# Two cross-attention prologues: the value projections of chunk 1 and its key casts move in among the row maxima of chunk 0, and the order of the clock-keeping matmuls changes

## The reference

```
q = layernorm(x) @ Wq + bq;  k = ctx @ Wk + bk;  v = ctx @ Wv + bv
attn = softmax(clip(q k^T * 16**-0.5, -1e4, 1e4))      # per head, over 12544 keys
x = x + (attn @ v) @ Wo + bo
```

## Time and profile before

| | us |
|---|---|
| median of three executions | 1392.23 |
| the profiled execution | 1387.69 |
| its span, first to last instruction | 1385.9 |
| TensorE busy in it | 1216.7 (88%) |
| VectorE, ScalarE, GpSimd busy | 716.0, 712.6, 224.6 |
| share of the chain that ended last: TensorE, VectorE, DMA | 73%, 16%, 5% |

### The profile page before, as it was taken

One profiled execution on the slowest core, in us unless ns is written; L12 is line 12 of the kernel. 1 busy time (PEld: TensorE's weight loads), 2 busy tenths in 40 slices (PEclk: granted clock), 3 DMA queues, 4 the chain that ended last, 5 costly groups with the idle time before them and its releaser, 6 DMA issues.

```text
span 1385.9 us, 29435 instructions
## 1 busy us (share of the span) xinstructions
PE 1216.7 (88%) x12725; PEld 784.6 (57%) x12725; DVE 716.0 (52%) x1348; ACT 712.6 (51%) x991; POOL 224.6 (16%) x118
## 2 busy tenths in 40 slices
PE   8799999999999988315899799999999999988556
PEld 6256666666666655315697256666566666555345
DVE  2546555555555563577222545555555555563431
ACT  3246666666666657152113256666666666657110
POOL 0222222222222200041000222222222222200000
PEclk9689999999999999558799799999999999999568
DMA  8969777777777660610706969777777777660803
GB/s 146 135 84 122 95 95 95 99 93 97 99 96 95 76 150 2 217 53 27 277 1 106 131 92 126 96 88 97 97 91 97 96 97 95 75 117 2 326 11 55
DMA packets 85155, 140.31 MB, mean 101 GB/s; under 512 B 9112, under 2 KB 76384, under 8 KB 84512
## 3 DMA queue, kind: packets, MB, share of 16 engines
q1 hardware_dynamic: 84128, 138.29, 63.9%
q10 hardware_dynamic: 896, 0.12, 0.1%
HBM read 60.05 MB, written 0.18 MB: 43 GB/s over the span
## 4 chain that ended last, share of the span: by engine, by line
PE 73%; DVE 16%; DMA 5%; issue 2%; ACT 2%; POOL 0%; SPq 0%; ACTq 0%; DVEq 0%; POOLq 0%
PE ring L547 40%; PE st L547 16%; PE ot L547 15%; DVE mpart L1202 8%; DMA qst<-rowb 3%; DVE arena L1329 2%; PE ring L678 1%; DMA arena<-scratch_perm 1%; DVE arena L1333 1%; ACT arena L921 1%; PE ring L553 0%; DMA warena<-ctxT 0%; PE ring L646 0%; DVE work L1323 0%; POOL arena L536 0%
## 5 line engine op out<-in xcount | busy, mean ns | idle before, releaser
L1202 DVE TENSOR_REDUCE mpart<-ring 128x1 f32<-128x448 f32 x896 | 516.7, 621 | 435.2 <-PE ring L547 432.8
L944 ACT ACTIVATE work<-st 128x1024 f32<-128x1024 f32 x392 | 400.8, 1022 | 197.7 <-PE st L547 193.1
L547 PE MATMUL ring<-arena,qst 96*128 96x448 bf16 x896 | 299.8, 369 | 4.9 <-DVE mpart L1202 2.7
L547 PE MATMUL st<-qst,arena 97*128 97x128 bf16 x3136 | 245.0, 221 | 19.5 <-DMA qst<-rowb 18.2
L547 PE MATMUL ot<-work,arena 128*17 128x128 f32 x6272 | 250.4, 277 | 8.9 <-issue 6.7
L547 PEld LDWEIGHTS st<-qst,arena 97*128 97x128 bf16 x3136 | 199.0, 99 | 84.3 <-issue 31.9
L547 PEld LDWEIGHTS ot<-work,arena 128*17 128x17 f32 x6272 | 138.5, 97 | 151.3 <-issue 103.7
L499 POOL TENSOR_TENSOR arena<-arena 128x896 f32<-128x896 f32 x52 | 98.2, 1888 | 715.6 <-ACT arena L917 715.6
L547 PE MATMUL ring<-warena,wkv 96*128 96x448 f32 x448 | 195.4, 566 | 2.0 <-DVE mpart L1202 1.3
L547 PE MATMUL ring<-wkv,warena 96*128 96x256 f32 x784 | 190.2, 385 | 0.9 <-DVE mpart L1202 0.8
L547 PEld LDWEIGHTS ring<-wkv,warena 96*128 96x128 f32 x784 | 147.4, 191 | 28.4 <-DVE mpart L1202 11.1
(11 more groups left out here) (269 smaller groups left out, 645.3 us busy)
## 6 DMA issues: line engine op xcount, KB each, us to landing
arena<-arena SPq DMA_DIRECT2D x336, 224.0 KB, 11.4
warena<-ctxT SPq DMA_DIRECT2D x28, 672.0 KB, 13.3
arena<-ffn_W SPq DMA_DIRECT2D x16, 1024.0 KB, 12.4
arena<-f SPq DMA_DIRECT2D x2, 4096.0 KB, 24.4
arena<-scratch_bc SPq DMA_DIRECT2D x1, 2048.0 KB, 6.7
arena<-scratch_perm SPq DMA_DIRECT2D x2, 1024.0 KB, 10.2
arena<-rows SPq DMA_DIRECT2D x1, 1792.0 KB, 7.0
warena<-w_in_proj SPq DMA_DIRECT2D x1, 1024.0 KB
```

Of the source, the lines that this page charges most:

```text
L547: return nc.tensor.matmul(o, l, r, start=start, stop=stop, **kw)
L944: nc.scalar.activation(pbuf[:, n % 2], st[:, 2 * (n % 2):2 * (n % 2) + 2].rearrange("p b k -> p (b k)"), ACT.Exp).then_inc(*signal(f"{lay} ...
L1202: V.reduce_max(mpart[:, 2 * h + hf:2 * h + hf + 1], ring[:, BANKS[step][0], 0:HALF], AX_X).then_inc(*signal(f"{lay}_b_max"))
```

## The change

Three edits. The number of warm-up matmuls becomes 4 ahead of the transposition in both layers (16 before); behind it 12 in L0 (2 before) and 2 in L1 (as before). In the list the value steps of chunk 1 and the casts of its keys, which stood ahead of all maxima of chunk 0, are placed behind 5, 10, 15 and 20 of these; the last cast is placed behind 24. The remaining maxima of chunk 0 (the eight left) follow as before.

```diff
-WARM = (16, 2)
+WARM = (4, 12)
...
-    plan += [("v", 0, n) for n in range(4)] + [("k", 1, n) for n in range(4)] + [("v", 1, n) for n in range(4)]
-    plan += [("k1", 1, 0), ("k1", 1, 1), ("k2", 1, 0), ("k2", 1, 1)]
+    plan += [("v", 0, n) for n in range(4)] + [("k", 1, n) for n in range(4)]
+    for part in ([("v", 1, 0), ("k1", 1, 0)], [("v", 1, 1), ("k2", 1, 0)], [("v", 1, 2)], [("v", 1, 3), ("k1", 1, 1)]):
+        plan += some(5, 0) + part
+    plan += some(4, 0) + [("k2", 1, 1)]
     plan += some(2 * H, 0) + [("row", 0, 0)] + [("k", 2, n) for n in range(3)] + score(0) + [("k", 2, 3)] + score(1)
...
                 keep_clock(WARM[0])
                 transpose2(xn, 0, f"{lay}_ln_normed", f"{lay}_xT_full")
-                keep_clock(WARM[1])
+                keep_clock(WARM[1] if lay == "L0" else 2)
```

## The result

The changed kernel is slower: 1397.3 us median of 11 runs (1390.21 to 1404.61) against 1391.83 of 11 runs of the kernel before, a ratio of 1.0046 with the interval 1.0028 to 1.0064. The forecast was 3.9 us faster; it came out some 6 us slower, above the range's end of 1393.2.

What follows compares the result with a forecast made beforehand. The prologues were bound by projections before the maxima, the maxima, and a 4 KB row transfer of 12.5 us. L0 -1.6 and L1 -2.3 gave -3.9: 1383.8 profiled, 1388.3 as the median; range 1384.5 to 1393.2.

Steps and rivals of the forecast that it cites:

- The start of the maxima: Chunk 0's first maximum in each prologue: at 32.0 in L0 and 760.2 in L1, after a wait for the stack.
- Its neighbours, nearly gapless, bring the clock back: L0's value groups among the maxima: one at half rate, 3.5 us instead of 1.75, the next at full rate again.
- part 1: Value groups of chunk 1 go among chunk 0's maxima: these end 0.4 us later in L0, 2.3 earlier in L1.
- Rival D: Chunk 0's maxima: value groups at half rate throughout, +8.2 us in all, 1400.4; chance 0.15.
- Hidden by 10 us: GpSimd's copy of `qst` ends near 56.5 instead of 52.8 in L0; first scores wait until 66 or later.
- part 2: Casts move with the value groups; with the row's landing, first scores come 1.6 us earlier in L0, 2.3 in L1.
- When only the first ten of the twelve are out: Row issued at 55.75 in L0 and 782.2 in L1, ahead of the stack's last transfers; L0's first scores 66.3.
- B: The row's transfer in both layers: it lands late whatever its issue, gain only 0.9 to 2 us, 1390.8; chance 0.15.
- A: The row's transfer overtakes two more stack transfers: another 3.8 us earlier in each layer, 1380.7; chance 0.08.
- Keep them fed until about 57: DMA engines in L0: context of chunk 2 and five stack transfers keep them busy; the stack lands when it did.
- Part 3: Warm-up of 4 matmuls, transposition, 12 matmuls: L0's queries start at 10.8 instead of 11.21, carried as 0.45 us earlier.
- C: L1's thinned warm-up: the clock falls, keys at half rate, +2.1 us there, 1390.2 in all; chance 0.12.

Runs made afterwards that it cites:

- f2: The kernel before with one added wait: GpSimd's copy of `qst` starts only when the merged maxima are there; ratio 1.0030.
- h1: The changed kernel with GpSimd's copy of `qst` held until the merged maxima are cast; ratio 1.0003.
- e2: The kernel before with only the new list of steps, its warm-up kept at 16 and 2; ratio 1.0079.
- h2: h1 with f1's unread matmuls in TensorE's wait ahead of the first maximum; ratio 0.9991.
- e3: The changed kernel with GpSimd's copy of `qst` moved ahead of the splitting of chunk 1; ratio 0.9972.
- e4: The changed kernel with the first cast of half 1 behind the second value group instead of the fourth; ratio 1.0014.
- f1: The changed kernel with unread identity matmuls, 8 in L0 and 4 in L1, ahead of the first maximum; ratio 1.0033.
- f3: The changed kernel with the moves of e3 and e4 together; ratio 1.0022.
- f4: The changed kernel with the copy of `qst` early and the first value group back ahead of all maxima; ratio 1.0020.
- g2: f4 with SP waiting for the row before it sends the last six transfers of stack(1); ratio 0.9849.
- g4: The changed kernel as it is, timed and profiled again; ratio 1.0063 against the kernel before.
- h3: The changed kernel with SP waiting for the row before it sends the last six transfers of stack(1); ratio 0.9935.

## Why the prediction was wrong

**The start of the maxima: right.** First maximum at 31.32 and 766.49, after 1.99 us of waiting for the stack; relative to the layer's start 5.4 and 5.9 us earlier than before, against 4.7 and 5.7 forecast.

**"Its neighbours, nearly gapless, bring the clock back" failed.** This is the step in part 1 where I took one half-rate group in L0. The fall came where I put it, but TensorE's records then filled 1.99 and 2.00 of 2.00 us in the windows at 32 and 44, and the clock was still at 0.50. It took until 49. Rival D's mechanism, in L0 alone: the maxima span 27.4 us (31.32 to 58.7) instead of 22.2. Of these 5.2, two more half-rate groups are 2 x (3.19 - 1.21) = 4.0; the rest is the size of a gap (1.21 instead of 1.0, 3.19 instead of 2.8, 0.35 instead of 0.1) and 0.34 us between the first maximum and the second. In L1 gaps of 1.21 are worth 1.0 us more than forecast. D's price for L0 was 4.6 us at the end of the maxima; it measured 4.9 (58.7 against 53.8).

**"Hidden by 10 us" failed.** This is the step in part 2 on the copy of `qst`. I asked who waits for the copy and found nobody before 66. I did not ask what runs beside it. Its end came 8.4 us later than before, on top of the merge, and VectorE's cast waited it out: 1.7 us in each layer, in a stretch where everything is on the path. f2 shows this cost alone, in the kernel before (1.0030), and h1 takes it alone out of the change (1.0003). The Trainium skill would have warned ("SBUF — State Buffer", section on who interferes with whom): a VectorE instruction with two SBUF inputs, or a copy or cast in a two-port mode, and a GpSimd instruction that reads SBUF exclude each other for the whole of the one that started first, and reductions stay clear. The trace agrees: `mdiff` (two inputs) 1.81 us in e2, `nmf` (a cast) 1.87 in the change; and in the kernel before the same copy ran from 50.92 to 52.81 beside the maxima, which are reductions and kept their rate (32 in 17.1 us).

**"When only the first ten of the twelve are out" failed as a consequence.** The delay made the row's issue 62.04, 0.3 us behind that of the last transfer, and 791.30 in L1, 0.3 behind as well. Without it (h1, h2) ten of the twelve were out, as forecast, and the row landed after 9.9 and 10.8 us in L0 where I had 10.5. So between the change and h1 the collision cost 3.3 and 4.0 us in the first scores, 7.2 together, of which 1.7 in each layer is the held cast; the timing says about 6 (1.0003 against 1.0046). That the remainder is the row's place in the queue is likely and not shown by these runs alone, since the row took 12.3 us in L1 of e3 with the same ten out. What the hold shows (3.2 us with six held back) is that the row lands by what is out ahead of it, as forecast, and not late whatever its issue (B). That it lands earlier still (A, 1.9 us for each of two transfers) doesn't fit L0, but L1 of h1 and h2, where it took 9.2 and 9.9 us and I had 12.6, comes near it. The round-robin between queues at packet granularity that I weighed from the Trainium skill ("DMA: Bandwidth & Descriptors", section on queues, rings and completion order) would by itself let the row pass the stack. That its completion came after 12.5 us in the kernel before, and after 3.2 with six transfers held back, shows that it doesn't. The rows show when a completion is seen and not when the data arrived, so they don't decide in which order the packets went.

**"Keep them fed until about 57" failed and cost little by itself.** The engines were idle from 53, since only five transfers were out and the other seven waited for a third part that was ready at 57.2. e4 ended the gap, and the row still took 11.3 us in L0 and 10.4 in L1.

**Part 3: right in its sign in L0** (queries at 9.8 instead of 11.2; I had 10.8, with 20 of the 24 records at 0.211 us, but all 24 took 3.5 us), **and C's mechanism is real**: in four of thirteen executions the keys of L1 lost 1.7 or 4.0 us. It was not what made this execution slow: its keys took 6.25 us.

The terms add up. L0's first scores are 7.5 us later than the forecast's 66.3: -0.7 at the start, +5.2 in the maxima, +1.8 in the merge, +1.2 in the row's transfer. L1's are 1.7 later relative to its start: -0.2, +1.0, +1.8 and -0.8. What the change was forecast to bring was nearly all there when both causes were gone (L0 of h2: -2.4 against -1.6; L1 had slow keys there, and with the collision alone removed, in h1, it came to -4.5 against -2.3), but the whole kernel is then 0.9991, no difference that can be told.

Open are the timed values of f1, f3 and f4, 4 to 6 us above what their first scores say. Open is also why L1's value groups fell to half rate in one of two executions of the changed kernel and, for the first group, in e4: TensorE had waited only 0.29 and 0.46 us before those maxima, so the long wait that goes with the fall in L0 is not its only cause.

## What to carry to other kernels

When a step moves later on a queue, look up what will run beside it at its new place and not only who waits for it: an operation with 10 us to spare can still stop the critical engine for its whole length, as the copy of `qst` did for 1.7 us. When work is taken off the path ahead of a wait, the engine now waits instead, and its clock may fall for what comes next. A filler (f1, h2) or a group left in front (f4, g2) kept it here, though f1 and f4 show no gain in the timing. Before an order on the engines is tuned around a small transfer, look at what stands ahead of it in the DMA queues: holding six large transfers back until the 4 KB one had landed was worth 1.65%, more than twice what the worst of the orders cost.

## What the runs showed of the hardware

- GpSimd's copy of 96x2048 bf16 inside SBUF (1.9 us) held VectorE's 128x16 operations: 1.81 to 1.87 us instead of 0.17, ending with the copy. It held a 128x896 subtraction for 2.67 us (1.09 for its neighbours), which ended 0.9 us behind the copy.
- After a wait of 1.99 us the clock fell to its lower level (1.2 GHz) within 1.1 us of the first maximum's matmul and stayed there for 17 us (32 to 49) with TensorE's records filling the time. All six executions with a wait of 1.76 to 2.26 us in L0 (the change, g4, e2, e4, h1, h3) had half-rate groups there. With the wait at 0.25 to 0.46 us (the early copy: e3, f3, g3), filled by matmuls (f1, h2) or by a group (f4, g2), no value group of L0 was at half rate; in L1 two executions had some after waits of 0.29 (g4) and 0.46 us (e4).
- A 4 KB transfer on its own queue took 10.4 to 12.6 us from issue to landing when twelve transfers of 224 KB and one of 672 KB had been issued ahead of it on another queue, 9.2 to 12.3 with ten of the twelve out, and at most 3.2 when six of them were held back.
